# First layer's gate weights: by selector matmuls into PSUM in place of a round trip through DRAM

## What is computed

```python
# "cond" FFN: 8 experts of width 64, top 2, and a shared expert of width 128
gp = leaky(einsum('th,ehm->etm', x, w_gate)); up = einsum('th,ehm->etm', x, w_up)
y_all = einsum('etm,emh->eth', gp * up, w_down)
y = sum_k topk_w[:, k] * y_all[topk_idx[:, k]] + (leaky(x @ sw_gate) * (x @ sw_up)) @ sw_down
# "ffn": 16 experts of width 64, top 4 of 2 groups, and a shared expert; weights scaled by 2.5
inter = silu(einsum('nh,ehm->enm', y, w_gate)) * einsum('nh,ehm->enm', y, w_up)
out = einsum('ne,enh->nh', combine, einsum('enm,emh->enh', inter, w_down)) + shared(y)
x = x + out
```

## Time and profile before

| | |
|---|---|
| three executions | 378.29, 379.27, 380.31 us; median 379.27 |
| the profiled execution | span 375.1 us from first to last instruction; its time outside the span is not listed on its own, the median of the three lies 4.2 us above the span |
| busy share of the span | PE 72%, DVE 69%, ACT 44%, POOL 43% |
| DMA | 20.87 MB, mean 56 GB/s |
| mean granted TensorE clock | 0.896 of full |

### The profile page before, as it was taken

One profiled execution on the slowest core, in us unless ns is written; L12 is line 12 of the kernel. 1 busy time (PEld: TensorE's weight loads), 2 busy tenths in 40 slices (PEclk: granted clock), 3 DMA queues, 4 the chain that ended last, 5 costly groups with the idle time before them and its releaser, 6 DMA issues.

```text
span 375.1 us, 5005 instructions
## 1 busy us (share of the span) xinstructions
PE 271.3 (72%) x1777; PEld 208.1 (55%) x1777; DVE 257.9 (69%) x441; ACT 165.0 (44%) x261; POOL 160.1 (43%) x177
## 2 busy tenths in 40 slices
PE   4575729879409985756658778765665999999984
PEld 3553415646309873644537555553554788887763
DVE  2249835694266879897556657652466999999994
ACT  2223501563200022544232243423979399999850
POOL 8985431000056310000054655652403857698852
PEclk9979959999958996698669999999889699999998
DMA  8940180000996400000000000008006600000001
GB/s 188 257 75 0 47 183 0 0 1 17 193 222 111 175 4 0 2 0 0 2 2 3 2 2 2 0 3 224 0 2 204 248 0 2 2 0 2 0 0 56
DMA packets 25751, 20.87 MB, mean 56 GB/s; under 512 B 10304, under 2 KB 20341, under 8 KB 25728
## 3 DMA queue, kind: packets, MB, share of 16 engines
q1 hardware_dynamic: 24864, 20.10, 21.2%
q0 software_dynamic: 864, 0.46, 1.3%
HBM read 19.84 MB, written 0.72 MB: 55 GB/s over the span
## 4 chain that ended last, share of the span: by engine, by line
PE 33%; DVE 28%; POOL 14%; DMA 10%; ACT 7%; issue 6%; SPq 1%; POOLq 0%; DVEq 0%
PE ps L779 9%; PE ps L780 8%; PE ps L781 8%; DMA arena<-comb_f 5%; PE ps L847 3%; POOL arena L533 2%; DMA arena<-comb_c 2%; POOL rstd L514 2%; POOL arena L524 2%; DVE n L1351 2%; DVE arena L1282 2%; DVE g_lo L1484 2%; DVE arena L1358 2%; DVE arena L1202 2%; DVE ssum L1411 1%
## 5 line engine op out<-in xcount | busy, mean ns | idle before, releaser
L779 PE MATMUL ps<-act_hi,w_hi 128*128 128x512 f32 x120 | 51.6, 430 | 26.0 <-ACT att_bias L763 7.5
L1484 DVE TENSOR_TENSOR g_lo<-att_bias,g_hi 128x1024 fp32r<-128x1024 f32 x32 | 59.0, 1878 | 1.3 <-ACT g_hi L769 0.7
L780 PE MATMUL ps<-act_lo,w_hi 128*128 128x512 f32 x120 | 49.0, 409 | 0.0
L781 PE MATMUL ps<-act_hi,w_lo 128*128 128x512 f32 x120 | 48.7, 406 | 0.0
L763 ACT ACTIVATE att_bias<-ps,vec 128x512 f32<-128x512 f32 x64 | 41.9, 686 | 10.2 <-PE ps L781 10.1
L779 PEld LDWEIGHTS ps<-act_hi,w_hi 128*128 128x128 f32 x120 | 23.9, 199 | 38.1 <-issue 29.8
L567 POOL TENSOR_TENSOR act_lo<-f_down,act_hi 128x512 fp32r<-128x512 f32 x16 | 28.0, 1750 | 28.9 <-ACT act_hi L726 28.8
L524 POOL TENSOR_TENSOR arena<-arena,smax 128x528 f32<-128x528 f32 x8 | 8.6, 1073 | 56.1 <-DVE smax L1404 56.1
L498 POOL TENSOR_TENSOR arena<-arena 128x512 f32<-128x512 f32 x6 | 10.2, 1730 | 52.1 <-DMA arena<-comb_f 52.1
L893 PE MATMUL ps<-f_down,arena 128*128 128x128 f32 x144 | 18.4, 293 | 14.1 <-DVE arena L1282 14.1
L590 POOL TENSOR_TENSOR k_diag<-k_diag 128x512 f32<-128x512 f32 x14 | 23.3, 1663 | 12.2 <-DVE k_diag L1518 12.2
(11 more groups left out here) (274 smaller groups left out, 667.9 us busy)
## 6 DMA issues: line engine op xcount, KB each, us to landing
arena<-comb_f SPq DMA_DIRECT2D x4, 1024.0 KB, 15.5
arena<-gate_m SPq DMA_DIRECT2D x8, 512.0 KB, 7.7
arena<-comb_c SPq DMA_DIRECT2D x4, 512.0 KB, 9.0
w_stage<-in_L_ffn_W SPq DMA_DIRECT2D x1, 2048.0 KB, 11.8
w_stage<-in_L_ffn_W SPq DMA_DIRECT2D x8, 256.0 KB, 4.4
x_tok<-in_x SPq DMA_DIRECT2D x2, 256.0 KB, 3.1
w_stage<-in_L_ffn_w_gate SPq DMA_DIRECT2D x1, 512.0 KB, 5.1
w_stage<-in_L_ffn_w_up SPq DMA_DIRECT2D x1, 512.0 KB, 5.5
```

What stands on the lines that cost most here:

```text
L779: pe.matmul(dst, wh, xh, start=first, stop=False)
L780: pe.matmul(dst, wh, xl, start=False, stop=False)
L781: return pe.matmul(dst, wl, xh, start=False, stop=last)
L1484: dve.tensor_tensor(g_lo[:, k % 2, b, :], gelu[:, k % 2, b, :], g_hi[:, k % 2, b, :].bitcast(f32), ALU.subtract).then_inc(v_glo, 1)
```

## The change

All four DRAM steps of the first layer's two FFNs go. In their place:

- `comb` is stored by token tile (`comb_tok` [128, tile, expert]); TensorE makes eight transposes of it (`gate_rows`) into banks 4 and 5, so that each expert's 1024 weights lie in one partition.
- ScalarE copies the rows as fp32r (`gate_rows_high`), VectorE forms the remainder (`gate_rows_low`).
- `gate_sel`, made once from the identity, selects a pair: `spread` multiplies it with the high and the low rows, two fp32r matmuls of 512 columns, into bank 4 or 5 in turn. That is the broadcast, 24 times in all.
- VectorE multiplies the hidden block with that bank (`weigh`), 24 times; POOL multiplies none.
- Spreads and weighs are placed by hand between units and between down matmuls. A spread waits for the weigh before the last one.
- `rp_rows` and `rp_h` move to memory of their own, which with the new tiles lies where `att_bias` comes later.

```diff
-            for s in range(HALVES):                               # SyncE, both FFNs
-                for e in range(2):
-                    sp.dma_start(f_gate[e * DH:(e + 1) * DH, :, s * HW:(s + 1) * HW],
...
-                for q in (5, 6, 7):                               # POOL
...
+            def gate_rows_high(n, s, rows):
+
+                act.wait_ge(pe_rows, 2 * n + s + 1)
+                act.activation(gate_hi[0:rows, s * HW:(s + 1) * HW], bank(4 + s)[0:rows, :], ACT.Copy)\
+                    .then_inc(act_gates, 1)
...
                 if CH_F + u < CH_N:
                     chunk(CH_F + u)
+                if u == 6:
+                    for s in range(HALVES):
+                        gate_rows_high(0, s, C_EXP)
...
+                if u == 2 * C_BLK + 10:
+                    act.wait_ge(pe_gate, 2 * C_PAIRS)
+                    for s in range(HALVES):
+                        gate_rows_high(1, s, F_EXP)
...
+            def gate_rows(n, rows):
+                pe.wait_ge(v_comb, n + 1)
+                pe.wait_ge(v_T, 2)
+                for s in range(HALVES):
+                    for t in range(HT):
+                        mm = pe.transpose(bank(4 + s)[0:rows, t * P:(t + 1) * P], comb_tok[:, s * HT + t, 0:rows],
+                                          ident[:, :])
+                    mm.then_inc(pe_rows, 1)
+
+            def spread(n, i, rows, pairs):
+
+                s, q = divmod(i, pairs)
+                done = (0, 2 * C_PAIRS)[n] + i
+                if i < 2:
+                    pe.wait_ge(v_gates, 2 * (n + 1))
+                if done >= 2:
+                    pe.wait_ge(v_mul, done - 1)
+                cols = slice(s * HW, (s + 1) * HW)
+                pe.matmul(bank(4 + i % 2), gate_sel[0:rows, q, :], gate_hi[0:rows, cols], start=True, stop=False)
+                pe.matmul(bank(4 + i % 2), gate_sel[0:rows, q, :], gate_lo[0:rows, cols], start=False, stop=True)\
+                    .then_inc(pe_gate, 1)
...
                 if u == 6:
-                    turn_gates(1, C_EXP * TILES)
+                    gate_rows(0, C_EXP)
+                if u >= 8:
+                    spread(0, 2 * (u - 8), C_EXP, C_PAIRS)
+                    spread(0, 2 * (u - 8) + 1, C_EXP, C_PAIRS)
...
-                    if b == 0:
-                        pe.wait_ge(v_mul, s + 1)
-                    if b == 3:
-                        pe.wait_ge(pool_mul, s + 1)
+                    else:
+                        pe.wait_ge(v_mul, C_PAIRS * s + b + 1)
                     mm = pe.matmul(bank(6 + s), c_down[:, b, :], c_hid[:, b, s * HW:(s + 1) * HW],
                                    start=(n == 0), stop=(n == C_BLK - 1))
+                    if s == 0 and n < C_PAIRS:
+                        spread(0, C_PAIRS + n, C_EXP, C_PAIRS)
...
                 if j == 10:
-                    turn_gates(2, P)
+                    pe.wait_ge(act_exp, 2)
+                    gate_rows(1, F_EXP)
+                if j >= 12:
+                    spread(1, j - 12, F_EXP, F_PAIRS)
...
+            for i in range(6, 10):
+                spread(1, i, F_EXP, F_PAIRS)
             for s in range(HALVES):
                 pe.wait_ge(v_hid, 2 * C_BLK + F_BLK * (s + 1))
-                pe.wait_ge(v_mul, 2 + s + 1)
-                pe.wait_ge(pool_mul, 2 + 3 * (s + 1))
+                pe.wait_ge(v_mul, 2 * C_PAIRS + F_PAIRS * (s + 1))
...
+                    if s == 0 and t < 3:
+                        spread(1, 10 + 2 * t, F_EXP, F_PAIRS)
+                        spread(1, 11 + 2 * t, F_EXP, F_PAIRS)
...
+            dve.tensor_copy(gate_sel[:, :, :].rearrange("p q (h m) -> p (q h) m", h=2),
+                            ident[0:F_EXP, 0:F_EXP].unsqueeze(2).broadcast_to([F_EXP, F_EXP, DH])).then_inc(v_sel, 1)
...
+            def weigh(n, i, hid, pairs, blocks):
+
+                s, q = divmod(i, pairs)
+                cols = slice(s * HW, (s + 1) * HW)
+                dve.wait_ge(pe_gate, (0, 2 * C_PAIRS)[n] + i + 1)
+                dve.wait_ge(v_hid, (0, 2 * C_BLK)[n] + blocks * s + q + 1)
+                dve.tensor_tensor(hid[:, q, cols], hid[:, q, cols], bank(4 + i % 2), ALU.mult).then_inc(v_mul, 1)
...
```

More of the change, by code:

```diff
@@ L165, in two_layers @@
         var_e = sb("var_e", [P, TILES])
+        with nc.sbuf_tensor("rp_early", [P, 7 * P], f32) as rp_early, \
+                nc.sbuf_tensor("gate_sel", [F_EXP, F_PAIRS, P], f32r) as gate_sel, \
+                nc.sbuf_tensor("gate_hi", [F_EXP, TOK], f32r) as gate_hi, \
+                nc.sbuf_tensor("gate_lo", [F_EXP, TOK], f32r) as gate_lo:
+            pass
+        att_bias = sb("att_bias", [P, TILES, HEADS, KEYS])
         with nc.sbuf_tensor("arena1", [P, 9216], f32) as arena1:
@@ L231, in two_layers @@
             "x", "small", "vec", "wc", "wf", "wq", "cd", "fd", "wo", "kv", "gk", "rp", "att", "null",
-            "comb_c", "gate_c0", "gate_c1", "comb_f", "gate_f0", "gate_f1", "bias_w", "bias_r", "w1", "w2",
+            "bias_w", "bias_r", "w1", "w2",
             "gate_mw", "out")}
@@ L260, in two_layers @@
         act_ghi = sem("act_ghi")
+        act_gates = sem("act_gates")
+        pe_rows = sem("pe_rows")
+        pe_gate = sem("pe_gate")
+        v_sel = sem("v_sel")
+        v_gates = sem("v_gates")
         pool_w2 = sem("pool_w2")
@@ L1154, in _, with gate_rows_low @@
             link(dve.reciprocal(r_inv[:, :], r_sum[:, :]))
-            dve.tensor_tensor(comb[:, 0:64].rearrange("p (e t) -> p t e", t=TILES), z, bc(r_inv[:, :]), ALU.mult)\
-                .then_inc(v_comb, 1)
+            dve.tensor_tensor(comb_tok[:, :, 0:C_EXP], z, bc(r_inv[:, :]), ALU.mult).then_inc(v_comb, 1)
             c_unit(3)
+            def gate_rows_low(n, rows):
+                for s in range(HALVES):
+                    cols = slice(s * HW, (s + 1) * HW)
+                    dve.wait_ge(act_gates, 2 * n + s + 1)
+                    dve.tensor_tensor(gate_lo[0:rows, cols], bank(4 + s)[0:rows, :],
+                                      gate_hi[0:rows, cols].bitcast(f32), ALU.subtract).then_inc(v_gates, 1)
+            def weigh(n, i, hid, pairs, blocks):
+                s, q = divmod(i, pairs)
+                cols = slice(s * HW, (s + 1) * HW)
+                dve.wait_ge(pe_gate, (0, 2 * C_PAIRS)[n] + i + 1)
+                dve.wait_ge(v_hid, (0, 2 * C_BLK)[n] + blocks * s + q + 1)
+                dve.tensor_tensor(hid[:, q, cols], hid[:, q, cols], bank(4 + i % 2), ALU.mult).then_inc(v_mul, 1)
             def rp_norm(n, sig):
@@ L1179, in _ @@
             dve.tensor_copy(vec[:, :], bank(7)[:, 128:128 + V_ROWS]).then_inc(v_small, 1)
[L1180 to L1181 removed]
+            gate_rows_low(0, C_EXP)
             c_unit(7)
@@ L1184, in _ @@
             c_unit(8)
+            weigh(0, 0, c_hid, C_PAIRS, C_BLK)
+            weigh(0, 1, c_hid, C_PAIRS, C_BLK)
             c_unit(9)
-            for s in range(HALVES):
-                dve.wait_ge(ld[f"gate_c{s}"], 32)
-                cols = slice(s * HW, (s + 1) * HW)
-                for q in range(3):
-                    dve.wait_ge(v_hid, C_BLK * s + q + 1)
-                    ins = dve.tensor_tensor(c_hid[:, q, cols], c_hid[:, q, cols], c_gate[:, q, cols], ALU.mult)
-                ins.then_inc(v_mul, 1)
+            for i in range(2, 2 * C_PAIRS):
+                weigh(0, i, c_hid, C_PAIRS, C_BLK)
             for s in range(HALVES):
@@ L1264, in _ @@
                 f_unit(u)
+                if u >= 12:
+                    weigh(1, u - 12, f_hid, F_PAIRS, F_BLK)
                 if u == 10:
@@ L1271, in _ @@
                         .then_inc(v_rp, 2)
-                if u == 11:
-                    dve.wait_ge(pe_comb, 2)
-                    dve.tensor_copy(comb_T[:, :], bank(5)[:, 0:P]).then_inc(v_combT, 1)
+                if u == 10:
+                    gate_rows_low(1, F_EXP)
             f_unit(16)
+            weigh(1, 4, f_hid, F_PAIRS, F_BLK)
             f_unit(17)
-            for s in range(HALVES):
-                cols = slice(s * HW, (s + 1) * HW)
-                dve.wait_ge(ld[f"gate_f{s}"], 32)
-                for q in range(5):
-                    dve.wait_ge(v_hid, 2 * C_BLK + F_BLK * s + q + 1)
-                    ins = dve.tensor_tensor(f_hid[:, q, cols], f_hid[:, q, cols], f_gate[:, q, cols], ALU.mult)
-                ins.then_inc(v_mul, 1)
+            for i in range(5, 2 * F_PAIRS):
+                weigh(1, i, f_hid, F_PAIRS, F_BLK)
             def norm_stats(s):
```

52 lines of the change are left out of this document (9 added, 43 removed).

## The result

The changed kernel takes 381.68 us (median of 12 executions, 379.96 to 383.17); the kernel before took 379.20 beside it (12 executions). The ratio is 1.0082, with a 95% interval from 1.0057 to 1.0107: slower by 0.8%, where 366.5 was forecast. The profiled execution took 380.53 us with a span of 378.7, against a span of 375.1 before. The time stands 1.8 us above the span of the same execution, so the profiled execution of before, at some 376.9 us (an estimate), was one of its faster ones; that is why the spans differ by 3.6 us and the medians by 2.5.

The account below looks back on a forecast made before the run. Bound taken: TensorE waiting on DMA bandwidth for the comb broadcasts, with slow-clock down matmuls after. Gains of 5.5 us (first stage) and 7.3 us (second) sum to 12.8: 379.3 - 12.8 = 366.5 us, range 363.5 to 370.5.

Parts of the forecast that it names:

- I take 0.46: Price in us of one spread, two fp32r matmuls of 512 columns at 0.23 each; high bound 1.7.
- with no hole there are no slow blocks: First stage's down product: without the DMA wait the clock stays up, 1.7 us of the 5.5 us gain.
- Stage 1: First stage: down product ends at 58.6 us instead of 64.1, a gain of 5.5 us.
- the 0.6 that I had named: First stage: VectorE's unit step with all inputs in SBUF, 1.26 us instead of 0.69 beside POOL at worst.
- Stage 2: Second stage: down product ends at 124.9 us instead of 132.2 on the old trace's clock, a gain of 7.3 us.
- (a): Second stage's tail: clock falls while spreads and weighs alternate, 1.7 us lost, 368.2 us; chance 0.16.
- the 0.21 that was to be its sign: Second stage's down half: instructions of 0.21 us would show that the clock fell in the tail.
- (b): Spreads: weight loads of 0.19 us show ahead of each matmul, 9.1 us come back, 375.6 us; chance 0.03.
- (c): All 24 spreads: each waits out its weigh, 1.5 us in place of 0.46, 25 us more, 391.5 us; chance 0.03.
- the 0.5 that was to be the sign of (c): TensorE idle over 0.5 us ahead of spreads, released by VectorE, would show that spreads wait out their weighs.
- (d): Kernel's end does not move, as something with a clock of its own ends last: 379.3 us; chance 0.02.

Follow-up runs that it names:

- full-row fillers: Changed kernel plus useless 128-row, 512-column matmuls where TensorE waits in both stages, spreads still 8 and 16 rows: 371.57 us, ratio 0.9802.
- six banks and few rows: Changed kernel with the last spreads of a stage also using the unit banks once free, rows still 8 and 16: 372.81 us, ratio 0.9839.

## Why the prediction was wrong

**The steps that failed.** "I take 0.46: operands fp32r and columns as in the unit; nothing excludes less below, but no row is cheaper per column." I priced the spread by columns and took the row count to be nothing, though I had written that no row has one with 8 or 16 contraction rows. And "with no hole there are no slow blocks": I made an idle TensorE the only thing that lowers the clock, because that was all the trace of before showed. The term of the sum that was mis-sized is the spread: priced at 0.46 us in a unit, it adds 0.86 at full clock (a unit of 2.24 us less six matmuls of 0.23), and it takes the clock from the down matmuls beside it. With the rows changed to 128 and nothing else, the forecast's picture appears:

- Span: forecast 362.3, measured 362.2 with all rows, 378.7 in the changed kernel.
- Second down product: forecast to start at 99.7 and end at 119.4; 100.09 and 119.5 with all rows; 111.4 and 136.3 in the changed kernel.

**Stage 1**, 9.9 us beyond the forecast (68.5 against 58.6). Of it 1.0 is another error: weigh 2 ends at 49.75, not 48.7, since unit 9's last steps on VectorE took longer than I had them. Half of it is the step with all inputs in SBUF, 1.17 us at 47.25, the 0.6 that I had named as what could be taken back and left out of the sum. The kernel with all rows has it too. The four rounds took 12.6 us instead of 5.4 (+7.2), and the second half's ten instructions 6.1 instead of 4.3 (+1.8), both at the low clock; that is the 9.9 to within 0.1. Not all of it is clock: at full clock four such rounds with few rows take 6.8 us (4 x 1.71), so of the 7.2 some 1.4 go with the changes of row count and 5.8 with the clock.

**Stage 2**, 7.0 us beyond (67.8 against 60.8). Units and tail took 1.8 more, with the slow gaps at each switch of rows; the first half of the down product 16.2 instead of 11.0 (+5.2), at the low clock; the second half 8.7 as forecast. With all rows this stage is 0.8 shorter than forecast, as a unit with its spread takes 1.84 and not 1.95, and that hides stage 1's 1.0: the agreement of 362.2 with 362.3 holds two errors of opposite sign, and is in part luck.

**The rivals.** (a) had the right thing, the clock, and in the second stage the right place: it falls in the tail, near 110 us, and the instructions of the first down tile take 4.21 / 18 = 0.23 us, near the 0.21 that was to be its sign. It had the first stage, the reason and the size wrong. It tied the fall to a thin stretch of 3.5 us and gave it 1.7 us, for 368.2; the fall came in both stages and lasted some 17 and 10 us. Most of the loss goes with it: the kernel with its clock kept by full-row fillers is through the second down product at 125.1 us, 11.2 before the changed kernel and 5.6 behind the one with all rows. The Trainium skill's account beside it (short idles between groups that cycle through PSUM) would have had me look at both stages; but as a cause it doesn't hold here. With every idle filled by few-row matmuls the clock fell, and with the idles left as they were (1.50 and 0.76 us before spreads, at 46.8 and 49.8) and all rows it stayed up. (b), weight loads that show, had half a point. Its price was 0.19 ahead of each spread matmul; measured are 0.2 us at each switch between 128 rows and 8, 16, 32 or 64, in two distances of 0.33, and nothing further behind a switch or with 96 rows. The Trainium skill's rule there ("TensorE: Matmul & The Clock Gate", section "The mechanism": a load overlaps a running matmul only if the row groups differ) disagrees with the trace: in the units matmuls of the same 128 rows start 0.23 us apart, with loads of 0.19 us out of sight. (The same section names a second case, a load into the background weight buffer; no run here tells whether that is what happens.) (c) did not happen as priced, 25 us: TensorE's idle ahead of spreads, released by weighs, is 2.9 us in all. But two of its four waits, 1.42 and 0.89 us, are over the 0.5 that was to be the sign of (c), so that sign alone was no proof. (d) did not either; the end moved, both ways.

**What held.** The weighs (684 ns, 0.69 forecast), eight transposes (1.03 us busy, forecast 0.9 to 1.0 net), no late load, the chain without comb, and the part behind the second down product, 242.4 us (242.9 before). The sign turned on the row count alone.

**Still open.** How the clock depends on rows between 64 and 96, and why one execution of four with 64 rows was 8 us shorter. What takes the 0.1 us in a distance at a switch, and why 96 rows against 128 don't have it: the row counts that keep the clock (96 and 128) are the same that keep the distances at 0.23, and no run tells whether the two have one cause. What makes the part behind the second down product 242.4 us in one execution and 244.5 in another. No kernel measured few-row matmuls apart from all other work.

## What to carry to other kernels

A matmul that contracts over a few rows (a selector, a broadcast, a rank-one term) set among full ones can pull TensorE's clock down for everything around it; fill its operands up with zeros to 128 partitions, which brought 16.5 us of span here at no visible cost: the spread behind unit 9's wait starts at 46.80 us with all rows and at 46.79 with 8. Read the granted clock beside the busy share: a TensorE that is busy 100% at 0.50 looks like a bound and is a loss. And when no row of the trace shows the shape that a change brings in, the unknown isn't its own duration only but what it does to its neighbours.

## What the runs showed of the hardware

- TensorE busy for 4.00 of 4.00 us with few-row matmuls in the mix, and the granted clock at 0.53 and 0.50 there; with the same number of fillers of 128 rows in their place it is 1.00. Zeros in the added rows are as good as data: both kernels with full rows, of zeros and of real weights, held it.
- Where TensorE changes between 128 rows and 8, 16, 32 or 64, two distances are 0.33 us in place of 0.23, the one across the change and the one behind it; with 96 rows against 128 they are 0.23 and 0.24. A switch there and back costs 0.4 us.
- Few rows don't always lower the clock: in the changed kernel's units, where two matmuls of 16 rows follow six of 128, it stays at 1.00 from 98 to 106 us.
- At the low clock spread matmuls of 8 rows follow each other by 0.43 us (49.31 to 49.74 in the kernel with six banks and few rows) against 0.23 to 0.24 at the full clock (43.16 to 43.40 in the changed kernel). A full-row matmul of as many columns takes the same 0.23 there, so in a row of its like a spread costs no more. Its effect on the clock and on the distances beside it is another.
